# Narrow attention's Newton steps and step orders: drains replaced by a chained semaphore, new orders on every engine

## The chip, the cores and the metric

One core of one Trainium2 chip. The metric is device time of one execution in microseconds (us), lower is better. The kernel before took 7786.44 us, the median of 3 runs (7783.06 to 7791.43).

## The reference, cut to what matters

The whole kernel is a stack of four mixer and feed blocks over 8 sequences of 512 tokens with 128 channels, float32. The change touches one of them, the feed of block 0 (names that begin with L0f in the profile): a local attention net of depth 6 with 16 heads of 64 channels and windows of 32 tokens. Cut down:

```python
def attn_layer(x, Wqkv, qs, ksc, Wo):
    q, k, v = split(x @ Wqkv)                 # 16 heads x 64 each
    q = q / max(norm(q), 1e-12) * qs          # also k
    q = q * cos * scale + rotate_half(q) * sin * scale
    k = k * cos / scale + rotate_half(k) * sin / scale
    out = local_attention(q, k, v)            # own and previous 32 tokens, softmax
    return out @ Wo

def ffn_layer(x, g, bln, W1, b1, W2, b2):
    xn = layernorm(x) * g + bln
    a, gate = split(xn @ W1 + b1)
    return a * gelu(gate) @ W2 + b2
```

Each layer's two halves are preceded by a shift of half the channels by one token, and each adds to x. The change touches how 1 / norm is reached (three Newton steps on an integer guess) and in which order everything is issued, not what is computed.

## The kernel before, in words

`narrow_attention_net` (L354) cuts a sequence into four tiles (tt = 0 to 3) of 128 tokens. One pass of the main stage handles one sequence of one layer: 6 layers by 8 sequences, 48 passes, written out without loops. Two short stages of the same code stand around it, one that fills the pipeline and one that empties it.

Every engine has an order of its own. TensorE's is written by hand: `ORDER` (L381) lists one tile's steps, `SIDE` (L385) puts the ten steps of the feed half and of the next sequence's input at one of three places, (tile, place), `tile_steps` expands both. A step of TensorE for tile tt works on different tiles of the data:

- `q`, `k` (i = 0 or 1): projection of 8 heads for tile tt + 2, L1110, two recorded matmuls. `v`: the same for tile tt + 1.
- `tq`, `tk`: four transposes (L1116) of the rotated and scaled q or k of tile tt + 1.
- `score` u: a mask matmul (L1129) and 64 small recorded matmuls (L1135). `flip` u: four transposes of the probabilities (L1143). `value` u: 64 small recorded matmuls (L1165). `oturn` u: four transposes of the result (L1171). `out`: 16 recorded matmuls with Wo (L1182). `value 1`, `oturn 1` and `out` are one tile behind.
- sides: `shift` (L1099) and `fshift` (L1191 to L1193), the shifted inputs of the two halves; `fturn` (L1198); `gate` and `up` 0 to 2 (L1205); `down` (L1211).

Steps of the kinds in `RING` write one of four PSUM banks in turn: a step's bank is that of the ring step four before it, and it waits until that one has been read out.

The other engines' orders are computed. `in_order` (L461) walks over TensorE's steps and adds up `TOOK`; each step calls for events on the other engines (`act_events`, `dve_events`, `pool_events`), and each event is due at its step's end plus a delay from `LATER` (main stage) or `PLAIN` (the other two). An engine's order is that of the due times, and within it each engine runs strictly in order.

What a q or k projection calls for: ScalarE copies it (L890) and squares it (L895); VectorE multiplies the swapped halves by sine, which also empties the PSUM bank (`rot`, L993), and sums the squares per head (`ssq`, L1001); GpSimd multiplies by cosine (`cos`, L849) and adds (`add`, L856). The buffers for the sine product and the squares are two deep. After a tile's last q or k comes `newton` (L1002 to L1017) on VectorE: eleven operations on 128 x 32 elements, each a true dependency of the one before it, with `e.drain()` ahead of each, and a count of the semaphore `normed` at the end. GpSimd then multiplies q and k by the result (`scale` 0 and 1, L862), for which the turns one tile later wait.

What a score calls for: `max` (L1022) and `sub` (L1027) on VectorE, the exponential on ScalarE (L918), `total` (L1033) with a reciprocal (L1036) on VectorE. `sub` waits for the count of `max`. What a value calls for: `onorm` (L1043) on VectorE, for which `oturn` waits. `fshift` calls for a copy and the statistics on VectorE (L1056 to L1062), `rstd` on GpSimd (L866 to L872) and `xn` on ScalarE (L936).

Of the kernel before, what the change touches and what calls it, by code (L numbers as in the profile page):

```python
# [9 lines left out]
I32 = mybir.dt.int32  # L10
# [343 lines left out]
def narrow_attention_net(nc, g, name, heads, depth, w):  # L354
# [19 lines left out]
    def turn(tt, what, c):  # L374
# [6 lines left out]
    ORDER = [("side", 0), ("value", 1), ("score", 0), ("q", 0), ("k", 1), ("oturn", 1), ("score", 1), ("q", 1), ("flip",  # L381
             0), ("out", 0), ("v", 1), ("k", 0), ("side", 1), ("value", 0), ("v", 0), ("tq", 0), ("side", 2), ("tk", 1),
             ("tq", 1), ("flip", 1), ("oturn", 0), ("tk", 0)]
    BEHIND = {("value", 0): 0, ("value", 1): 1, ("oturn", 0): 0, ("oturn", 1): 1, ("out", 0): 1}
    SIDE = [(("fshift",), (0, 1)), (("fturn",), (1, 1)), (("gate", 0), (1, 2)), (("gate", 1), (1, 2)), (("gate", 2), (2,  # L385
            0)), (("up", 0), (2, 2)), (("shift",), (0, 2)), (("up", 1), (2, 0)), (("up", 2), (2, 1)),
            (("down",), (3, 0))]
# [90 lines left out]
    def dve_events(step, D):  # L478
        kind = step[0]
        if kind == "proj" and step[2] != "v":  # L480
            found = [(D["rot"], ("rot",) + step[1:]), (D["ssq"], ("ssq",) + step[1:])]
            if step[2:] == QK_ORDER[-1]:
                found.append((D["newton"], ("newton", step[1])))
            return found
# [10 lines left out]
    def pool_events(step, D):  # L495
# [10 lines left out]
        if kind == "fshift":  # L506
# [3 lines left out]
    PLAIN = {"exp": 1.5, "unflip": 0.3, "ocopy": 0.3, "xn": 2.0, "act_ring": 0.2, "copy": 0.2, "square": 1.0, "ssq": 2.0, "rot": 1.2, "newton":  # L510
             3.0, "max": 0.2, "sub": 0.2 + 0.6, "total": 5.0, "onorm": 0.5, "norm_gap": 2.0, "unflip_dve": 0.5, "dve_ring": 0.3, "cos": 1.0, "add": 2.5,
             "scale": 6.0, "scale_gap": 2.0, "rstd": 2.0}
    LATER = {"exp": 4.11, "unflip": 1.88, "ocopy": 1.76, "xn": 9.48, "act_ring": 1.83, "copy": 2.05, "square": 2.48,
             "ssq": 3.92, "rot": 3.52, "newton": 9.41, "max": 1.06, "sub": 3.3, "total": 5.73, "onorm": 4.32, "norm_gap":
             14.0, "unflip_dve": 6.64, "dve_ring": 1.85, "cos": 3.51, "add": 4.27, "scale": 11.99, "scale_gap": 0.54,
             "rstd": 4.39}
# [3 lines left out]
    with ExitStack() as ctx:  # L520
# [58 lines left out]
        def programs(r, STEPS):  # L579
# [7 lines left out]
            for _, tt, what, c in QK:  # L587
                assert place["ssq", tt, what, c] < place["newton", tt]
# [17 lines left out]
            made_by = lambda steps, kind: [s[1:] for s in steps if s[0] == kind]  # L606
            until_layer = lambda steps: steps[:steps.index(("layer",))] if ("layer",) in steps else []
# [3552 lines left out]
```

## Time and profile before

| what | value |
|---|---|
| median of 3 runs | 7786.44 us |
| profiled execution | 7796.52 us |
| its span | 7794.6 us |
| main stage of the narrow attention | from about 668 us to 4240 us |
| TensorE busy, whole span | 82% |
| VectorE, ScalarE, GpSimd busy | 73%, 55%, 60% |

The profile is one execution, seen instruction by instruction. PE is TensorE (PEld its weight loads), DVE VectorE, ACT ScalarE, POOL GpSimd, SP the engine that issues the DMAs. Each engine executes in its order, so the time between two starts on an engine is the price of the first with all its waits; a matmul's recorded end is modelled, and matmuls overlap, so starts are the surer reading. L numbers are lines of the kernel before.

### The profile page before, as it was taken

How to read it: one execution, taken by the hardware profiler on the slowest of the kernel's cores; microseconds unless marked ns; L12 is line 12 of the kernel's file. 1: busy time of each engine (PE TensorE's matmuls, PEld its weight loads, DVE VectorE, ACT ScalarE, POOL GpSimd, SP SyncE). 2: the span in 40 equal slices, each digit the busy share in tenths (PEclk: the TensorE clock that was granted, in tenths of full speed). 3: DMA queues.
4: the chain of work that ended last, by engine and by line, in shares of the span. 5: the costliest groups of instructions: out<-in, count | busy, mean ns of one | idle time of the engine just before them, and what ended most of it. 6: DMA issues, size and time to landing. Idle time of an engine off the chain costs nothing. (4 is left out here: it accounts for less than half of the span.)

```text
span 7794.6 us, 241834 instructions
## 1 busy us (share of the span) xinstructions
PE 6366.5 (82%) x93078; PEld 4343.4 (56%) x93078; DVE 5662.3 (73%) x11712; ACT 4278.5 (55%) x7973; POOL 4672.3 (60%) x3762
## 2 busy tenths in 40 slices
PE   5776999999999999999998599977888757734268
PEld 2333666666666666666665588874555423322256
DVE  6885888888887888888886477766777668853533
ACT  5553666666666666666665344436777655512012
POOL 5776777777777777777776254544444357723000
PEclk8888999999999999999999799999999978867579
DMA  3332112112112112112111200001110033333001
GB/s 116 123 135 57 50 47 66 47 51 64 48 51 60 51 47 63 50 50 61 50 51 39 70 6 6 6 20 27 23 31 23 17 134 126 132 121 87 10 14 33
DMA packets 344463, 440.90 MB, mean 57 GB/s; under 512 B 151976, under 2 KB 235648, under 8 KB 324416
## 3 DMA queue, kind: packets, MB, share of 16 engines
q1 hardware_dynamic: 335632, 405.19, 17.0%
q8 instruction: 759, 12.44, 0.7%
q10 hardware_dynamic: 1584, 15.21, 0.5%
q0 software_dynamic: 6144, 5.25, 0.4%
q14 instruction: 344, 2.82, 0.1%
HBM read 217.42 MB, written 42.14 MB: 33 GB/s over the span
## 5 line engine op out<-in xcount | busy, mean ns | idle before, releaser
L1110 PE MATMUL L0f_ring<-L0f_wqkv,L0f_hT 128*128 128x512 f32 x2324 | 1196.5, 624 | 20.5 <-issue 18.0
L849 POOL TENSOR_TENSOR L0f_qr<-L0f_qs,L0f_table 128x512 f32<-128x512 f32 x776 | 990.8, 1277 | 216.7 <-issue 115.1
L856 POOL TENSOR_TENSOR L0f_qr<-L0f_qr,L0f_m 128x512 f32<-128x512 f32 x776 | 989.3, 1275 | 138.0 <-issue 119.6
L862 POOL TENSOR_TENSOR L0f_qr<-L0f_qr,L0f_rn 128x1024 f32<-128x1024 f32 x388 | 752.0, 1959 | 422.3 <-DVE L0f_rn L1016 400.3
L890 ACT ACTIVATE L0f_qs<-L0f_ring 128x512 f32<-128x512 f32 x776 | 460.1, 593 | 625.0 <-PE L0f_ring L1110 618.1
L993 DVE TENSOR_TENSOR L0f_m<-L0f_ring,L0f_table 128x512 f32<-128x512 f32 x776 | 531.4, 685 | 46.2 <-ACT L0f_qs L890 14.5
L1001 DVE TENSOR_REDUCE L0f_ssq<-L0f_sq 128x8 f32<-128x512 f32 x776 | 528.1, 681 | 29.6 <-ACT L0f_sq L895 13.7
L1110 PEld LDWEIGHTS L0f_ring<-L0f_wqkv,L0f_hT 128*128 128x128 f32 x2324 | 382.1, 190 | 266.9 <-issue 210.5
L895 ACT ACTIVATE L0f_sq<-L0f_qs 128x512 f32<-128x512 f32 x776 | 492.0, 634 | 36.0 <-DVE L0f_ssq L1001 4.2
L1116 PEld LDWEIGHTS L0f_ring<-const_ident,L0f_qr 128*128 128x128 f32 x3088 | 361.8, 141 | 178.2 <-issue 170.5
L1116 PE MATMUL L0f_ring<-const_ident,L0f_qr 128*128 128x128 f32 x3088 | 428.2, 274 | 16.6 <-POOL L0f_qr L862 16.6
L1022 DVE TENSOR_REDUCE L0f_mx<-L0f_scores 128x8 f32<-128x512 f32 x384 | 265.6, 692 | 165.5 <-PE L0f_scores L1135 160.5
L1182 PE MATMUL L0f_ring<-L0f_wo,L0f_oT 128*128 128x128 f32 x3088 | 382.5, 277 | 2.9 <-issue 2.1
L2475 PE MATMUL L0a_y<-L0a_hc,const_ident 128*128 128x512 f32 x512 | 288.6, 698 | 108.3 <-DVE L0a_hc L2396 86.7
L1165 PEld LDWEIGHTS L0f_scores<-L0f_vmix,L0f_pT 64*32 64x32 f32 x18480 | 264.7, 105 | 190.8 <-issue 185.0
L1182 PEld LDWEIGHTS L0f_ring<-L0f_wo,L0f_oT 128*128 128x128 f32 x3088 | 362.2, 193 | 10.0 <-issue 3.6
L1135 PE MATMUL L0f_scores<-L0f_kT,L0f_qT 64*32 64x64 f32 x24576 | 337.3, 224 | 36.9 <-issue 36.9
L2475 PE MATMUL L2a_y<-L2a_hc,const_ident 128*128 128x512 f32 x512 | 283.5, 687 | 101.3 <-DVE L2a_hc L2396 85.1
L904 ACT ACTIVATE L0f_vb<-L0f_ring 128x512 f32<-128x512 f32 x386 | 230.5, 597 | 246.7 <-PE L0f_ring L1110 246.4
L2255 POOL TENSOR_TENSOR L0a_dbu<-L0a_du,L0a_bc_all 128x512 f32<-128x512 f32 x256 | 325.3, 1304 | 57.1 <-DVE L0a_du L2375 50.2
L2255 POOL TENSOR_TENSOR L2a_dbu<-L2a_du,L2a_bc_all 128x512 f32<-128x512 f32 x256 | 325.3, 1304 | 54.6 <-DVE L2a_du L2375 50.7
L1165 PE MATMUL L0f_scores<-L0f_vmix,L0f_pT 64*32 64x64 f32 x18480 | 324.2, 224 | 34.4 <-SPq L155 10.3
(533 smaller groups left out, 17157.9 us busy)
## 6 DMA issues: line engine op xcount, KB each, us to landing
L0f_vmix<-L0f_vb SPq DMA_DIRECT2D x768, 128.0 KB
L0a_bc_all<-L0a_bc_rows SPq DMA_DIRECT2D x32, 2048.0 KB, 11.2
L2a_bc_all<-L2a_bc_rows SPq DMA_DIRECT2D x32, 2048.0 KB, 11.0
L0f_vmix<-L0f_vb SPq DMA_DIRECT2D x672, 64.0 KB
L1f_vmix<-L1f_vb SPq DMA_DIRECT2D x96, 128.0 KB, 2.3
L0f_wqkv<-L_ffn_wqkv_dram SPq DMA_DIRECT2D x7, 1536.0 KB, 6.0
L2f_parts<-L2f_zero ACTq DMA_DIRECT2D x8, 1088.0 KB, 12.7
n_s<-mixer_out SPq DMA_DIRECT2D x32, 256.0 KB, 4.9
```

The lines of the kernel that those rows point to most:

```text
L849: e.tensor_tensor(rotated, qs[:, q % QN], spread(cos, 1, 8), ALU.mult).then_inc(cosed.sem, 1)
L856: e.tensor_tensor(rotated, rotated, m2[:, q % SN], ALU.add).then_inc(added.sem, 1)
L862: e.tensor_tensor(rotated, rotated, spread(rn[:, tt, 2 * c:2 * c + 2], 3, DH), ALU.mult).then_inc(scaled.sem, 1)
L895: e.activation(sq[:, q % SN], qs[:, q % QN], ACT.Square).then_inc(squared.sem, 1)
L993: e.tensor_tensor(m2[:, q % SN].rearrange("p h (a d) -> p h a d", a=2), swapped, spread(sin, 1, 8).rearrange("p h (a d) -> p h a d", a=2), ...
L1001: e.tensor_reduce(ssq[:, tt % 2, slot(step)], sq[:, q % SN], AX.X, ALU.add).then_inc(summed.sem, 1)
L1110: e.matmul(bank[:], hT[:, buffer_of(it, step), tt * P:tt * P + P], wqkv[:, layer % 2, col:col + 512], start=True, stop=True).then_inc(full, 1)
L1116: a = e.transpose(bank[:, j * P:j * P + P], qr[:, tt % 2, 2 * c + "qk".index(what), 2 * j:2 * j + 2, :], g.ident[:])
L1165: a = e.matmul(o_ps[cols, s, h, j], pT[half, s, j, cols], values, start=True, stop=True)
L1182: a = e.matmul(bank[:, 0:C], oT[:, tt % 2, j, :], wo[:, j, :], start=j == 0, stop=j == pairs - 1)
L2255: e.tensor_tensor(dbu[:, s], du[:, par, d], bc_all[:, n // QN, 0, n % QN], ALU.mult).then_inc(dbu_ready.sem, 1)
L2475: e.matmul(y_ps[:, d], g.ident[:], hc[:, (2 * n + d) % 4], start=n == 0, stop=n == states - 1).then_inc(added.sem, 1)
```

## The change

The eleven operations of `newton` become eleven steps, each with a due time of its own (`newton` plus i times `newton_gap`), so that other steps of VectorE can fall between them. The drains go: step i waits for the count that step i - 1 leaves in the new semaphore `stepped`, step 0 for the tile's last `ssq`; step 10 counts `normed`. `ORDER`, `SIDE` and the delays `LATER` are replaced.

```diff
-    ORDER = [("side", 0), ("value", 1), ("score", 0), ("q", 0), ("k", 1), ("oturn", 1), ("score", 1), ("q", 1), ("flip",
-             0), ("out", 0), ("v", 1), ("k", 0), ("side", 1), ("value", 0), ("v", 0), ("tq", 0), ("side", 2), ("tk", 1),
-             ("tq", 1), ("flip", 1), ("oturn", 0), ("tk", 0)]
+    ORDER = [("value", 1), ("side", 0), ("k", 1), ("score", 0), ("q", 0), ("oturn", 1), ("score", 1), ("v", 1), ("q", 1),
+             ("flip", 0), ("out", 0), ("k", 0), ("side", 1), ("value", 0), ("v", 0), ("flip", 1), ("tq", 0), ("tk", 0),
+             ("side", 2), ("oturn", 0), ("tq", 1), ("tk", 1)]
-    SIDE = [(("fshift",), (0, 1)), (("fturn",), (1, 1)), (("gate", 0), (1, 2)), (("gate", 1), (1, 2)), (("gate", 2), (2,
-            0)), (("up", 0), (2, 2)), (("shift",), (0, 2)), (("up", 1), (2, 0)), (("up", 2), (2, 1)),
-            (("down",), (3, 0))]
+    SIDE = [(("fshift",), (0, 2)), (("fturn",), (1, 1)), (("gate", 0), (2, 0)), (("gate", 1), (2, 0)), (("gate", 2), (2,
+            0)), (("up", 0), (2, 1)), (("shift",), (0, 1)), (("up", 1), (2, 1)), (("up", 2), (2, 1)), (("down",), (2, 2))]
...
-                found.append((D["newton"], ("newton", step[1])))
+                found += [(D["newton"] + D["newton_gap"] * i, ("newton", step[1], i)) for i in range(11)]
...
-    LATER = {"exp": 4.11, "unflip": 1.88, "ocopy": 1.76, "xn": 9.48, "act_ring": 1.83, "copy": 2.05, "square": 2.48,
-             "ssq": 3.92, "rot": 3.52, "newton": 9.41, "max": 1.06, "sub": 3.3, "total": 5.73, "onorm": 4.32, "norm_gap":
-             14.0, "unflip_dve": 6.64, "dve_ring": 1.85, "cos": 3.51, "add": 4.27, "scale": 11.99, "scale_gap": 0.54,
-             "rstd": 4.39}
+    LATER = {"exp": 3.43, "unflip": 2.66, "ocopy": 2.24, "xn": 8.29, "act_ring": 2.88, "copy": 0.93, "square": 2.98,
+             "ssq": 4.36, "rot": 2.48, "newton": 5.91, "newton_gap": 0.22, "max": 1.12, "sub": 1.55, "total": 4.54,
+             "onorm": 2.65, "norm_gap": 14.0, "unflip_dve": 6.33, "dve_ring": 1.0, "cos": 5.86, "add": 5.9, "scale": 13.61,
+             "scale_gap": 4.95, "rstd": 1.96}
...
-            normed = r.count("normed", made_by(DVE_STEPS, "newton"))
+            stepped = r.count("stepped", [s for s in made_by(DVE_STEPS, "newton") if s[1] < 10])
+            normed = r.count("normed", [s[:1] for s in made_by(DVE_STEPS, "newton") if s[1] == 10])
...
-                            tt = step[1]
+                            tt, i = step[1:]
                             flat = lambda t: t.rearrange("p c h -> p (c h)")
                             z, t, out = flat(ssq[:, tt % 2]), flat(est[:]), flat(rn[:, tt])
-                            e.drain()
-                            e.tensor_scalar(z, z, 1e-24, None, ALU.max)
-                            e.drain()
-                            e.tensor_scalar(out.bitcast(I32), z.bitcast(I32), -0.5, float(0x5F3759DF), ALU.mult, ALU.add)
-                            for i in range(3):
-                                e.drain()
-                                e.scalar_tensor_tensor(t, out, -0.5, out, ALU.mult, ALU.mult)
-                                e.drain()
-                                e.tensor_tensor(t, t, z, ALU.mult)
-                                e.drain()
+                            if i:
+                                e.wait_ge(*stepped(it, (tt, i - 1)))
+                            else:
+                                e.wait_ge(*summed(it, LAST_SSQ[tt]))
+                            if i == 0:
+                                a = e.tensor_scalar(z, z, 1e-24, None, ALU.max)
+                            elif i == 1:
+                                a = e.tensor_scalar(out.bitcast(I32), z.bitcast(I32), -0.5, float(0x5F3759DF), ALU.mult, ALU.add)
+                            elif i % 3 == 2:
+                                a = e.scalar_tensor_tensor(t, out, -0.5, out, ALU.mult, ALU.mult)
+                            elif i % 3 == 0:
+                                a = e.tensor_tensor(t, t, z, ALU.mult)
+                            else:
                                 a = e.scalar_tensor_tensor(out, t, 1.5, out, ALU.add, ALU.mult)
-                            a.then_inc(normed.sem, 1)
+                            a.then_inc(normed.sem if i == 10 else stepped.sem, 1)
```

## Rows read from the trace of the kernel before

**Rows 1.** Busy by window: start:end, length, PE, PEld, DVE, ACT, POOL, PE clock, DMA
```profile
2000.00:3000.00 1000.00, 955.39 (x17970) 657.60 (x17969) 818.24 (x1819) 674.29 (x1226) 781.47 (x592) 1.00 0.19 52
```

**Rows 2.** Instructions on tile hT: ns min/median/max, first to last start
```profile
L885 ACT ACTIVATE L0f_hT<-L0f_ring x49: 598/599/601, 634.5 to 4178.3; 128x512 f32<-128x512 f32 x49
```

**Rows 3.** Waits of PE, 760 to 4170 us: total us, times, longest us
```profile
PE L0f_ring L1099 <- DVE L0f_m L993: 40.9, 46, 1.2
PE L0f_scores L1135 <- issue: 34.6, 27, 2.2
PE L0f_scores L1143 <- ACT L0f_prob L918: 22.6, 44, 0.8
```

**Rows 4.** Timeline of PE in one pass: start, us, instruction [idle before]
```profile
853.05 1.13 PE L1110 MATMUL L0f_ring<-L0f_wqkv,L0f_hT 128*128 128x512 f32 x2
854.01 0.60 PE L1116 MATMUL L0f_ring<-const_ident,L0f_qr 128*128 128x128 f32 x4
855.48 0.66 PE L1099 MATMUL L0f_ring<-const_ident,L0f_xs 128*128 128x128 f32 x4 [0.87 <-DVE L0f_m L993]
...
857.28 0.60 PE L1171 MATMUL L0f_ring<-const_ident,L0f_os 128*128 128x128 f32 x4
857.72 0.60 PE L1116 MATMUL L0f_ring<-const_ident,L0f_qr 128*128 128x128 f32 x4
859.40 0.38 PE L1129 MATMUL L0f_scores<-L0f_mask,ident_bf 128*128 128x256 bf16 x2
859.71 0.86 PE L1135 MATMUL L0f_scores<-L0f_kT,L0f_qT 64*32 64x64 f32 x64
860.50 1.98 PE L1110 MATMUL L0f_ring<-L0f_wqkv,L0f_hT 128*128 128x512 f32 x4
862.32 0.60 PE L1171 MATMUL L0f_ring<-const_ident,L0f_os 128*128 128x128 f32 x4
```

**Rows 5.** Timeline of PE later in the same pass, to the next pass's fshift
```profile
882.82 1.12 PE L1110 MATMUL L0f_ring<-L0f_wqkv,L0f_hT 128*128 128x512 f32 x2
884.46 0.66 PE L1143 MATMUL L0f_scores<-const_ident,L0f_prob 128*128 128x128 f32 x4 [0.51 <-ACT L0f_prob L918]
...
916.52 0.63 PE L1171 MATMUL L0f_ring<-const_ident,L0f_os 128*128 128x128 f32 x4
...
921.27 1.88 PE L1110 MATMUL L0f_ring<-L0f_wqkv,L0f_hT 128*128 128x512 f32 x4
923.31 0.67 PE L1191 MATMUL L0f_ring<-f,const_ident 128*128 128x256 f32 x2 [0.15 <-DVE f L1051]
```

**Rows 6.** Timeline of DVE, the last Newton operation of a tile and what follows
```profile
914.94 0.19 DVE L1016 SCALAR_TENSOR_TENSOR L0f_rn<-L0f_est,L0f_rn 128x32 f32<-128x32 f32 x1
915.09 0.69 DVE L1022 TENSOR_REDUCE L0f_mx<-L0f_scores 128x8 f32<-128x512 f32 x1
915.69 0.68 DVE L1043 TENSOR_TENSOR L0f_os<-L0f_scores,L0f_sums 128x512 f32<-128x512 f32 x1
```

**Rows 7.** Groups of DVE, 760 to 4170 us: count, busy us, mean ns, idle before
```profile
L1012 DVE SCALAR_TENSOR_TENSOR L0f_est<-L0f_rn 128x32 f32<-128x32 f32 x555 | 188.3, 339 | 44.5 <-issue 3.6
L1036 DVE RECIPROCAL L0f_sums<-L0f_sums 128x8 f32<-128x8 f32 x370 | 75.2, 203 | 34.4 <-issue 0.9
```

**Rows 8.** Timeline of ACT, a copy and the square that waits for it
```profile
923.25 0.60 ACT L890 ACTIVATE L0f_qs<-L0f_ring 128x512 f32<-128x512 f32 x1 [0.26 <-PE L0f_ring L1110]
923.94 0.63 ACT L895 ACTIVATE L0f_sq<-L0f_qs 128x512 f32<-128x512 f32 x1
```

**Rows 9.** Timelines of DVE and ACT: fshift's copy, the next rot, and xn
```profile
924.84 0.69 DVE L1056 COPY L0f_xn<-L0f_ring 128x512 f32<-128x512 f32 x1 [0.79 <-PE L0f_ring L1193]
...
927.14 0.69 DVE L993 TENSOR_TENSOR L0f_m<-L0f_ring,L0f_table 128x512 f32<-128x512 f32 x1 [0.19 <-issue]
...
932.76 1.65 ACT L936 ACTIVATE L0f_xn<-L0f_xn,L0f_shifted,L0f_rstd 128x128 f32<-128x128 f32 x4 [1.06 <-POOL L0f_shifted L872]
```

**Rows 10.** Waits of POOL, 760 to 4170 us: total us, times, longest us
```profile
POOL L0f_qr L862 <- DVE L0f_rn L1016: 384.5, 176, 4.3
```

More of the change, by code:

```diff
@@ L508, in pool_events @@
         return []
-    PLAIN = {"exp": 1.5, "unflip": 0.3, "ocopy": 0.3, "xn": 2.0, "act_ring": 0.2, "copy": 0.2, "square": 1.0, "ssq": 2.0, "rot": 1.2, "newton":
-             3.0, "max": 0.2, "sub": 0.2 + 0.6, "total": 5.0, "onorm": 0.5, "norm_gap": 2.0, "unflip_dve": 0.5, "dve_ring": 0.3, "cos": 1.0, "add": 2.5,
+    PLAIN = {"exp": 1.5, "unflip": 0.3, "ocopy": 0.3, "xn": 2.0, "act_ring": 0.2, "copy": 0.2, "square": 1.0, "ssq": 2.0, "rot": 1.2, "newton": 3.0, "newton_gap": 0.01, "max": 0.2, "sub": 0.2 + 0.6, "total": 5.0, "onorm": 0.5, "norm_gap": 2.0, "unflip_dve": 0.5, "dve_ring": 0.3, "cos": 1.0, "add": 2.5,
              "scale": 6.0, "scale_gap": 2.0, "rstd": 2.0}
-    LATER = {"exp": 4.11, "unflip": 1.88, "ocopy": 1.76, "xn": 9.48, "act_ring": 1.83, "copy": 2.05, "square": 2.48,
-             "ssq": 3.92, "rot": 3.52, "newton": 9.41, "max": 1.06, "sub": 3.3, "total": 5.73, "onorm": 4.32, "norm_gap":
-             14.0, "unflip_dve": 6.64, "dve_ring": 1.85, "cos": 3.51, "add": 4.27, "scale": 11.99, "scale_gap": 0.54,
-             "rstd": 4.39}
+    LATER = {"exp": 3.43, "unflip": 2.66, "ocopy": 2.24, "xn": 8.29, "act_ring": 2.88, "copy": 0.93, "square": 2.98,
+             "ssq": 4.36, "rot": 2.48, "newton": 5.91, "newton_gap": 0.22, "max": 1.12, "sub": 1.55, "total": 4.54,
+             "onorm": 2.65, "norm_gap": 14.0, "unflip_dve": 6.33, "dve_ring": 1.0, "cos": 5.86, "add": 5.9, "scale": 13.61,
+             "scale_gap": 4.95, "rstd": 1.96}
     RING = ("shift", "proj", "turn", "oturn", "out", "fshift", "fturn", "gate", "up", "down")
@@ L587, in programs @@
             for _, tt, what, c in QK:
-                assert place["ssq", tt, what, c] < place["newton", tt]
+                assert place["ssq", tt, what, c] < place["newton", tt, 0]
                 assert place["cos", tt, what, c] < place["add", tt, what, c]
@@ L606, in programs @@
             made_by = lambda steps, kind: [s[1:] for s in steps if s[0] == kind]
+            LAST_SSQ = {s[0]: s for s in made_by(DVE_STEPS, "ssq")}
             until_layer = lambda steps: steps[:steps.index(("layer",))] if ("layer",) in steps else []
```

## The prediction

> **What bounds the kernel now.** TensorE is busy 82% of the span, but that is a mean over stages. I read first the window in the middle of the stage that the change touches: TensorE 95.5% busy, VectorE 82%, GpSimd 78%, ScalarE 67%, with TensorE's clock fully granted, its upper level of 2.4 GHz [rows 1]. The stage is 48 passes; between the first and the last copy of hT lie 48 of them and 3543.8 us, so 73.83 us a pass [rows 2], and a microsecond in the pass is 48 in the kernel. Then the waits of TensorE over 46 passes [rows 3], and the timeline of one pass for what they really cost, from start to start [rows 4, 5].
>
> What the reader is to see in the starts. After four transposes the next step starts 0.44 us later (857.28 to 857.72). The shift starts 1.47 after such a group (854.01 to 855.48), so it lost 1.03 [rows 4]; 46 waits, one a pass [rows 3]. Its bank is that of projection k0, which VectorE empties only behind fshift's copy and statistics (924.84 to 927.14, one pass on) [rows 9]. Value 1 stands directly behind turn k0 and too soon behind flip 1, and score 0 waits for turn k0's copy: 857.72 + 0.44 + 0.79 (64 small matmuls, 859.71 to 860.50) is 858.95, yet the mask matmul starts at 859.40, 0.45 lost [rows 4]. Tile 0 begins in the same way, so I count 0.8 a pass. A single projection ahead of transposes takes 0.96 (853.05 to 854.01), a double one 1.82 (860.50 to 862.32) [rows 4]. So flip 0 of tile 2, at 884.46 instead of 882.82 + 0.96, lost 0.68, waiting for an exponential [rows 5]; 44 waits say once a pass [rows 3]. fshift starts 2.04 after a double projection (921.27 to 923.31) instead of 1.82, behind the output's addition: 0.22 lost [rows 5]. And inside the small matmuls of score stand 27 holes without a releaser, 34.6 us in 46 passes, 0.75 a pass, up to 2.2 us each [rows 3]. Together 3.5 of 73.83.
>
> The holes stand only in score, the densest part of TensorE's program. The Trainium skill, Runtime: NRT & Kernel Launch, section Instruction fetch mechanics, says that fetching is hidden because instructions are dispatched more slowly than they are refilled. By that density is not their cause and they would all stay, which is one end of my term below; no row here names their cause.
>
> **The drains.** A small operation of the chain takes 0.19 us [rows 6] and has 0.08 idle ahead of it (44.5 us over 555) [rows 7]: 0.27 apart. In the new chain each waits for a count of the same engine instead; the trace does not show that for these operations. Lower end: independent long operations start 0.60 apart at 0.69 long (915.09 to 915.69), an overlap of 0.09 [rows 6], which a dependency should exclude. Nearest row: ScalarE's square, which waits for its copy by a count and starts 0.09 after it ends (923.25 + 0.60 to 923.94) [rows 8]. I take 0.09 against 0.08: 44 operations a pass, 0.4 us more of VectorE; the lower end would be 44 times 0.17, 7.5 less. So the drains' removal gains nothing. The Trainium skill, VectorE: DVE Perf Modes, section Rules for kernel authors, advises saving operations and not semaphores in a chain, since the flush comes anyway; by that rule too this part is worth 0.
>
> **The spreading.** I worked out VectorE's new order from ORDER, TOOK and LATER. Eleven due times 0.22 apart are 2.2 wide and meet hardly anything: in tile 0 fshift falls between the second and third step, in tile 2 onorm 0 between the fourth and fifth, in tiles 1 and 3 all eleven stand together. So the spreading is there in name only. It would not be on TensorE's path either: the chain ends before GpSimd's scale, which waited 384.5 us for it [rows 10], and the turns use scale's result most of a tile later. What it costs: max and sub now stand together with a wait between, where onorm or rot lay between them: 8 pairs a pass at 0.09 + 0.09, 1.4 us more of VectorE.
>
> **TensorE's order, taken away.** Shift comes right after k0; its bank is v1's, which ScalarE empties early: 1.03 gone. Five steps now part flip 1 from value 1, and score 0 has a projection ahead: 0.8 gone. fshift is far behind the output's addition: 0.22 gone. For flip 0 of tile 2, k1 and v1 now lie between the gates and it, but all three gates come at once on ScalarE: half of 0.68, 0.34. Value 1 and score 0, 260 small instructions in a row, are parted by k1: of the holes' 0.75 between nothing and all goes, I take half, 0.38. Together 2.8.
>
> **Added.** By 0.96 and 1.82 a second projection in a row costs 0.86, so each change from projection to transposes is 0.10 [rows 4]. Pairs q0 k1 and v1 k0 are split and v1 q1 is joined: one change more a tile, 0.4 a pass. A projection ahead of the mask matmul is in no row; 0 and 0.15 are its ends, 0.10 the nearest. Net 2.4.
>
> **VectorE's lateness.** A tile of TensorE without sides is some 14.7 us (11 to 12 in projections, transposes and scores as above, and two values and the output). VectorE's tile: 16 long operations at 0.60 [rows 6], 9.6; two reciprocals at 0.20 with a gap of 0.09 on either side [rows 7], 0.9 with what they keep from overlapping; the output's addition, 0.2; Newton, 11 times 0.27 and what slow ones add (L1012 alone 0.15 in the mean, three times a tile [rows 7]), about 4; two subs, 0.3: 15.0. The sides now pile up in tile 2 (gates, ups, down: some 8 us of TensorE for 4 of VectorE), and tiles 3, 0 and 1 run bare: TensorE 44.1 + 2.3 = 46.4, VectorE 45.0 + 2.3 for fshift [rows 9] = 47.3. Before, down and two gates lay in tiles 3 and 1. To that comes ScalarE: xn takes 1.65 and waited 1.06 for GpSimd [rows 9]; fshift moves 3.5 us later on TensorE, and behind ssq and two Newton steps on VectorE, xn only behind one copy more. Copies and squares queue behind that wait, rot and ssq behind them: 0.5 to 1. So VectorE falls 1.4 to 1.9 behind by tile 1. Its slack: today oturn 1 starts at 916.52, as soon as onorm 1 is done at 916.37 [rows 5, 6]; in the new order onorm comes ahead of max, which gives back 0.6. I charge 1.0 of new wait on oturn 1, between 0 and 2.
>
> GpSimd stays covered: busy 58 of 73.8 us a pass [rows 1], with 8 of waiting for Newton to give up [rows 10].
>
> **Sum.** 2.4 - 1.0 = 1.4 a pass, times 48: 67 us. The profiled execution took 7796.52, so 7729; the median stood 10 below it, so 7719.
>
> **Rivals.**
> 1. All goes well: no new wait, all of 0.68 and of the holes gone: 1.03 + 0.8 + 0.22 + 0.68 + 0.75 - 0.4 = 3.1, times 48 = 148: 7638. For it: TensorE hangs on VectorE by few links. Against: three bare tiles. Chance 0.13.
> 2. The orders only move the waits: 2.4 a pass of new ones, 7786. The drains alone would give this too, 0.4 us of VectorE being nothing. Chance 0.13.
> 3. Slower, by VectorE at the step from tile 0 to 1. fshift stands inside the Newton chain; if it is late the chain waits, onorm 1 and rot k1 come after it, and oturn 1 stops TensorE. It decides from 2.4 us of new wait. Small operations are sometimes slow; the mean of L1012 is 0.15 above 0.19 [rows 6, 7], which one in six at 1.1 would make (an estimate). Two such in tiles 0 and 1 each make 3.6, less 1.1 that the slack of tile 2 and the holes take back, plus my 1.0: 3.5, so 1.1 times 48 = 53: 7839. For it: GpSimd lags more when scale 1 is put between later steps. Against: tile 2 lets VectorE recover 3 us. Chance 0.24.
>
> The forecast has 0.50.
>
> **How the numbers follow.** A measurement of this kernel can tell 0.2% (16 us) from no change. Forecast and rival 1 are faster: 0.63; rival 2 is within: 0.13; rival 3 slower: 0.24. The forecast's own range is 7680 (new wait 0.2) to 7770. For 8 in 10 it reaches from 7650, near rival 1, to 7830, most of rival 3.
>
> **What would show it.** Right: the wait of L1099 on L993 gone, those of L1143 and L1165 smaller, new waits of L1171 on L1043, a pass of 72.4 us, Newton operations still 0.27 apart. Wrong: Newton chains cut by long operations or under 2.8 us; as many holes in L1135 as before; L1143 waiting over 1 us in tile 1; a pass over 74 us. If TensorE's waits vanish and the pass stays, my prices from start to start are wrong.

## The result, and the profile after

The kernel after takes 7588.7 us, the median of 4 runs (7580.1 to 7590.9), against 7788.9 us beside it on the same chip: ratio 0.974, 95% interval 0.9723 to 0.9757. The forecast was 7719 with a range of 7650 to 7830, so the time lies below the range, and below the best rival (7638).

The profiled execution took 7590.9 us with a span of 7588.9. The lines are those of before, with numbers three higher: L1113 is the projection, L1119 the turns, L1138 score, L1146 flip, L1168 value, L1174 oturn, L1194 to L1196 fshift; on VectorE L1011 to L1019 are Newton, L1025 max, L1030 sub, L1046 onorm, L1054 the output's addition, L1059 fshift's copy, L1077 and L1081 the feed's last two additions.

The instructions on tile hT, as in [rows 2] (min/median/max ns, first to last start):

```profile
L885 ACT ACTIVATE L0f_hT<-L0f_ring x49: 577/579/597, 634.2 to 3983.3; 128x512 f32<-128x512 f32 x49
```

The difference of the two starts is 3349.1 us over 48 passes, 69.77 us a pass where it was 73.83. That is 4.06 less, and 48 times this is 195 of the 200 us. So nearly all of it comes from the one stage. The window of [rows 1] (columns: length, PE, PEld, DVE, ACT, POOL, granted clock, DMA share, GB/s):

```profile
2000.00:3000.00 1000.00, 996.60 (x19160) 699.43 (x19159) 912.60 (x1929) 715.96 (x1302) 827.12 (x629) 1.00 0.21 58
```

TensorE is busy 99.7% of it (95.5% before) and VectorE 91% (82%): more passes lie in the window, and more of VectorE's small operations are slow (below). All waits of TensorE from 760 to 3960 us, the view of [rows 3] (total us, times, longest us):

```profile
PE L0f_scores L1138 <- issue: 3.0, 9, 0.5
PE L0f_ring L1174 <- DVE L0f_os L1046: 2.1, 7, 0.6
PE L0f_scores L1146 <- ACT L0f_prob L918: 1.4, 5, 0.3
PE L0f_ring L1113 <- ACT L0f_qT L911: 0.3, 1, 0.3
```

Together 7 us, where the whole list of before, of which [rows 3] show three, sums to 125: the shift's wait (40.9), the flips' (22.6) and the holes (34.6) of [rows 3] are gone but for 4.4 us, and the wait of oturn on onorm that I charged at 1.0 us a pass is 2.1 us in all. TensorE's timeline in a pass (start, us) shows the one cost that was added:

```profile
2002.31 1.13 PE L1113 MATMUL L0f_ring<-L0f_wqkv,L0f_hT 128*128 128x512 f32 x2
2003.28 0.38 PE L1132 MATMUL L0f_scores<-L0f_mask,ident_bf 128*128 128x256 bf16 x2
```

Here a projection ahead of the mask matmul takes 0.97 from start to start, 0.11 more than the 0.86 of a projection ahead of another; over all 184 of the stretch the mean is 0.94, 0.08 more. The forecast had 0.10. VectorE's timeline, with one line of GpSimd's, shows what the chained semaphore does:

```profile
2004.85 0.68 DVE L1025 TENSOR_REDUCE L0f_mx<-L0f_scores 128x8 f32<-128x512 f32 x1
2005.56 0.70 DVE L1030 TENSOR_TENSOR L0f_scores<-L0f_scores,L0f_mx 128x512 f32<-128x512 f32 x1
...
2014.98 1.27 POOL L856 TENSOR_TENSOR L0f_qr<-L0f_qr,L0f_m 128x512 f32<-128x512 f32 x1 [0.16 <-issue]
2015.11 1.20 DVE L1015 SCALAR_TENSOR_TENSOR L0f_est<-L0f_rn 128x32 f32<-128x32 f32 x1
2016.34 0.19 DVE L1017 TENSOR_TENSOR L0f_est<-L0f_est,L0f_ssq 128x32 f32<-128x32 f32 x1
2016.56 0.19 DVE L1019 SCALAR_TENSOR_TENSOR L0f_rn<-L0f_est,L0f_rn 128x32 f32<-128x32 f32 x1
2016.79 0.19 DVE L1015 SCALAR_TENSOR_TENSOR L0f_est<-L0f_rn 128x32 f32<-128x32 f32 x1
...
2030.54 0.18 DVE L1013 TENSOR_SCALAR L0f_rn<-L0f_ssq 128x32 int32<-128x32 int32 x1
2032.06 0.69 DVE L1059 COPY L0f_xn<-L0f_ring 128x512 f32<-128x512 f32 x1 [1.34 <-PE L0f_ring L1196]
2032.84 0.87 DVE L1062 BATCH_NORM_STATS2 L0f_stats<-L0f_xn 128x6 f32<-128x128 f32 x4
...
2034.28 0.23 DVE L1015 SCALAR_TENSOR_TENSOR L0f_est<-L0f_rn 128x32 f32<-128x32 f32 x1
```

Small Newton operations start 0.22 to 0.23 apart, not 0.27: each starts 0.03 us after the one it waits for ends. The same 0.03 stands between max and the sub that waits for its count. fshift's copy and statistics stand inside the chain, behind its second step. What my expectations below call fshift's addition is this group.

The first Newton operation shown takes 1.20 us, not 0.19. It begins while GpSimd's addition (L856) runs and ends some 0.05 after it (2015.11 + 1.20 = 2016.31, against 2014.98 + 1.27 = 2016.25). That is the rule in the whole trace: of the 2134 Newton operations of after, 336 take over 0.5 us, every one of them began while a multiplication by cosine (L849) or that addition (L856) of GpSimd was running, and each ended 0.035 to 0.054 us after it. None of the 1022 that overlap nothing of GpSimd's is slow. In before it is 246 of 2134, with 0.034 to 0.056. So the slow form reads as a wait for GpSimd's instruction to end, and it counts as busy: the 91% hold this waiting.

### The profile page after: what moved, and what is told of

It is laid out like the page before. It is cut to its first block and busy times, and to the rows that moved or that the text cites. A ratio compares the mean times of both kernels' runs of the same rounds, so it can differ in the third digit from the quotient of the medians.

```text
span 7588.9 us, 239593 instructions
## 1 busy us (share of the span) xinstructions
PE 6306.7 (83%) x93014; PEld 4349.8 (57%) x93078; DVE 5801.0 (76%) x11712; ACT 4272.6 (56%) x7973; POOL 4662.0 (61%) x3762
## 5 line engine op out<-in xcount | busy, mean ns | idle before, releaser
L1113 PE MATMUL L0f_ring<-L0f_wqkv,L0f_hT 128*128 128x512 f32 x2324 | 1236.0, 628 | 15.9 <-issue 10.8
L849 POOL TENSOR_TENSOR L0f_qr<-L0f_qs,L0f_table 128x512 f32<-128x512 f32 x776 | 988.2, 1273 | 141.1 <-issue 89.6
L856 POOL TENSOR_TENSOR L0f_qr<-L0f_qr,L0f_m 128x512 f32<-128x512 f32 x776 | 988.7, 1274 | 125.8 <-issue 123.2
L1113 PEld LDWEIGHTS L0f_ring<-L0f_wqkv,L0f_hT 128*128 128x128 f32 x2324 | 369.1, 190 | 208.4 <-issue 132.8
L1119 PE MATMUL L0f_ring<-const_ident,L0f_qr 128*128 128x128 f32 x3088 | 402.1, 273 | 16.7 <-POOL L0f_qr L862 16.7
L1119 PEld LDWEIGHTS L0f_ring<-const_ident,L0f_qr 128*128 128x128 f32 x3088 | 350.4, 141 | 18.4 <-issue 18.4
L1168 PEld LDWEIGHTS L0f_scores<-L0f_vmix,L0f_pT 64*32 64x32 f32 x18480 | 267.9, 106 | 140.8 <-issue 140.4
L1168 PE MATMUL L0f_scores<-L0f_vmix,L0f_pT 64*32 64x64 f32 x18480 | 330.7, 224 | 16.5 <-SPq L155 9.8
L1138 PE MATMUL L0f_scores<-L0f_kT,L0f_qT 64*32 64x64 f32 x24576 | 333.5, 224 | 3.3 <-issue 3.0
L1168 PE MATMUL L0f_scores<-L0f_vb,L0f_pT 64*32 64x64 f32 x6160 | 333.6, 225 | 0.0
```

The costliest lines, as they stand in the source:

```text
L849: e.tensor_tensor(rotated, qs[:, q % QN], spread(cos, 1, 8), ALU.mult).then_inc(cosed.sem, 1)
L856: e.tensor_tensor(rotated, rotated, m2[:, q % SN], ALU.add).then_inc(added.sem, 1)
L1113: e.matmul(bank[:], hT[:, buffer_of(it, step), tt * P:tt * P + P], wqkv[:, layer % 2, col:col + 512], start=True, stop=True).then_inc(full, 1)
L1119: a = e.transpose(bank[:, j * P:j * P + P], qr[:, tt % 2, 2 * c + "qk".index(what), 2 * j:2 * j + 2, :], g.ident[:])
L1168: a = e.matmul(o_ps[cols, s, h, j], pT[half, s, j, cols], values, start=True, stop=True)
```

## The experiments

Each ratio is to the kernel before on the same chip, with its 95% interval; "pass" is from the instructions on hT as above. A waits view of an experiment covers 760 to 3960 us, some 43 to 46 passes. ORDER and SIDE also set the due times, so an edit of either reorders the other engines too; the first two edits below, of drains and chain alone, leave every engine's order as it was. Line numbers differ by up to five between kernels; the tile names tell which line is meant.

| kernel | median us | ratio | pass us |
|---|---|---|---|
| after | 7588.7 | 0.9740 (0.9723 to 0.9757) | 69.77 |
| after, with drains | 7669.4 | 0.9841 (0.9823 to 0.9859) | 71.22 |
| before, with the chain | 7815.6 | 1.0028 (1.0018 to 1.0037) | 74.35 |
| the same, last addition from PSUM | 7788.0 | 0.9983 (0.9974 to 0.9993) | 73.60 |
| after, with the old delays | 7755.3 | 0.9952 (0.9934 to 0.9970) | 73.18 |
| before, with chain and new delays | 7816.7 | 1.0023 (1.0012 to 1.0033) | 74.21 |
| before, shift and fshift moved | 7769.2 | 0.9962 (0.9949 to 0.9974) | 73.12 |
| before, k 1 between value 1 and score 0 | 7893.2 | 1.0125 (1.0108 to 1.0142) | 75.89 |
| after, with the old sides | 7733.4 | 0.9918 (0.9899 to 0.9938) | 72.61 |
| after, score 0 ahead of k 1 | 7700.3 | 0.9866 (0.9850 to 0.9881) | 72.00 |
| after, reciprocals chained too | 7589.8 | 0.9727 (0.9714 to 0.9741) | 69.74 |
| after, gap 0 | 7764.0 | 0.9957 (0.9941 to 0.9974) | 73.29 |
| after, gap 0.8 | 7764.4 | 0.9958 (0.9942 to 0.9975) | 73.19 |
| after, gap 0, fshift ahead of the chain | 7658.0 | 0.9817 (0.9797 to 0.9838) | 71.06 |
| after, gap 0, fshift and onorm 20 ahead | 7618.1 | 0.9763 (0.9742 to 0.9784) | 70.23 |

**The drains put back.** Orders, sides and delays of after; only the chain's waits are replaced:

```diff
-                            if i:
-                                e.wait_ge(*stepped(it, (tt, i - 1)))
-                            else:
-                                e.wait_ge(*summed(it, LAST_SSQ[tt]))
+                            e.drain()
```

> The changed kernel with a drain ahead of each of the eleven Newton steps in place of the semaphore chain; all orders stay. In the profile after, a chained step starts 0.03 us after the one before it ends, a drained one before started 0.08 after: 44 steps a pass, 2 us of VectorE. Theory A (TensorE's new path made the gain, VectorE still idles 2.6 us a pass): 7589 to 7625 us. Theory B (VectorE is so full that the cheaper chain carries the gain): the 2 us come back on TensorE's path, 48 times, 7670 to 7690.

7669, at the lower edge of theory B's range. The waits of TensorE, first row, and below it the group of the Newton operation that [rows 7] show:

```profile
PE L0f_ring L1171 <- DVE L0f_os L1043: 47.5, 60, 1.5
```

```profile
L1012 DVE SCALAR_TENSOR_TENSOR L0f_est<-L0f_rn 128x32 f32<-128x32 f32 x540 | 229.9, 426 | 56.3 <-issue 11.1
```

The same group in the kernel after:

```profile
L1015 DVE SCALAR_TENSOR_TENSOR L0f_est<-L0f_rn 128x32 f32<-128x32 f32 x552 | 236.3, 428 | 22.9 <-issue 0.2
```

Idle ahead of each is 0.10 us with drains (56.3 over 540) and 0.04 with the chain (22.9 over 552), at an equal mean of 0.43 us busy. With drains oturn 1 waits 47.5 us for onorm, 1.06 a pass over the 45 in this stretch, in the place and of the size that the forecast charged. From start to start it costs a little more: the four projections of a pass that stand ahead of oturn 1 take 5.28 us with drains and 3.95 with the chain, and these 1.33 are most of the 1.45 between the two passes (71.22 and 69.77). So the chain is worth 80 us (7669.4 - 7588.7) on these orders, and nine tenths of it are this one wait.

**The chain alone.** Orders and old delays of before, the chain with gap 0.

```diff
-                            e.drain()
+                            e.wait_ge(*stepped(it, (tt, i - 1)))
```

> The semaphore chain alone: TensorE's order, the sides and the delays are those of before, with the eleven steps due at one time. Theory A: TensorE's waits of before (shift, value, score, flip) don't hang on the Newton chain, so 7770 to 7789 us. Theory B: 2 us of VectorE a pass are worth up to 96 us, 7690 to 7720.

It is 0.28% slower, which neither theory had. Lines of its timeline:

```profile
890.16 3.76 POOL L863 TENSOR_TENSOR L0f_qr<-L0f_qr,L0f_rn 128x1024 f32<-128x1024 f32 x2 [3.18 <-DVE L0f_rn L1020]
891.75 0.69 DVE L1078 TENSOR_TENSOR L0f_y<-L0f_ring,L0f_b 128x512 f32<-128x512 f32 x1 [1.67 <-PE L0f_ring L1215]
892.53 1.93 DVE L1082 TENSOR_TENSOR f<-L0f_y,f 128x512 f32<-128x512 f32 x1
895.16 0.68 DVE L1047 TENSOR_TENSOR L0f_os<-L0f_scores,L0f_sums 128x512 f32<-128x512 f32 x1
895.99 0.63 PE L1175 MATMUL L0f_ring<-const_ident,L0f_os 128*128 128x128 f32 x4 [0.46 <-DVE L0f_os L1047]
```

Newton ends sooner, GpSimd's scale starts sooner, and one of its two multiplications now runs when the feed's last addition begins. This adds two tiles in SBUF and takes 1.93 us instead of 0.69. onorm and oturn behind it are late: oturn waits 20.2 us in all, 0.47 a pass. The instructions on tile f, min/median/max ns, of the kernel before and of this one:

```profile
L1078 DVE TENSOR_TENSOR f<-L0f_y,f x49: 691/694/1834, 750.8 to 4276.3; 128x512 f32<-128x512 f32 x49
```

```profile
L1082 DVE TENSOR_TENSOR f<-L0f_y,f x49: 691/1928/1935, 746.6 to 4300.3; 128x512 f32<-128x512 f32 x49
```

**The same with one operand in PSUM.** This kernel leaves out the bias b2: its last addition reads the bank in PSUM instead of the tile y in SBUF. The addition into y still runs, and the bank is given free one addition later (the lines shown leave this out).

```diff
-                            e.tensor_tensor(x2, y[:], x2, ALU.add).then_inc(x2_ready.sem, 1)
+                            e.tensor_tensor(x2, ring.at(step).rearrange("p (t c) -> p t c", t=TT), x2,
+                                            ALU.add).then_inc(x2_ready.sem, 1)
```

> The chain alone on the orders of before, but the feed half's last addition reads its sum from PSUM and not from a second tile in SBUF (it leaves out the bias b2). With the chain alone that addition took 1.93 us instead of 0.69, since Newton ended sooner and the addition then met GpSimd's second scale, and oturn 1 of tile 3 waited 0.6 us longer. Theory D (two SBUF operands beside GpSimd make it slow): the addition takes 0.7 us, the wait of oturn (L1175) on onorm falls from 20 us to under 5, and the kernel is back at 7770 to 7795 us. Rival E (any operation beside scale is slow, or the wait has another cause): 1.9 us again and 7805 to 7825.

The last addition's instructions on tile f:

```profile
L1082 DVE TENSOR_TENSOR f<-L0f_ring,f x49: 690/692/692, 744.5 to 4263.6; 128x512 f32<-128x512 f32 x49
```

No instance is slow any more though GpSimd's multiplication runs beside 48 of the 49, no wait of oturn on onorm is left, and 0.45% comes back: theory D. The Trainium skill, GPSIMD Engine Reference, section Specifications, says that GpSimd's path to SBUF is shared with VectorE and contended by instructions with two SBUF inputs; this pair agrees, 1.93 us against 0.69. The traces also show the size. The 48 slow additions of the kernel with the chain alone, the 14 of before and 48 of the 49 in after end 0.544 to 0.549 us after the multiplication of GpSimd that ran when they began; the 34 quick ones of before began with only 0.13 or 0.14 of it left. So the price is the rest of GpSimd's instruction, and a different start makes it anything from nothing to 1.2 us. In after it is paid in full, where it holds up nothing:

```profile
L1081 DVE TENSOR_TENSOR f<-L0f_y,f x49: 693/1836/1840, 744.9 to 4081.7; 128x512 f32<-128x512 f32 x49
```

**The order alone.** ORDER and SIDE of after with the chain, but the LATER of before, a gap of 0 among them.

```diff
-             "ssq": 4.36, "rot": 2.48, "newton": 5.91, "newton_gap": 0.22, "max": 1.12, "sub": 1.55, "total": 4.54,
...
+             "ssq": 3.92, "rot": 3.52, "newton": 9.41, "newton_gap": 0.0, "max": 1.06, "sub": 3.3, "total": 5.73, "onorm": 4.32, "norm_gap":
...
```

> TensorE's new order and sides with the old delays, so that VectorE, ScalarE and GpSimd are ordered by the delays of before. Theory A in its strong form (TensorE's order alone): 7589 to 7620 us. Rival C (the delays matter, since fshift's statistics and max stand ahead of what TensorE waits for): half of the gain is lost, 7660 to 7740, with new waits of oturn (L1174) on onorm.

All of its waits of TensorE:

```profile
PE L0f_ring L1174 <- DVE L0f_os L1046: 86.1, 175, 1.3
PE L0f_scores L1146 <- ACT L0f_prob L918: 14.2, 44, 0.8
PE L0f_scores L1168 <- ACT L0f_pT L923: 13.3, 43, 0.7
PE L0f_scores L1138 <- issue: 1.6, 6, 0.3
```

Shift, fshift and the holes are mended, and four oturns a pass wait for onorm instead: 86 us. It went theory C's way, and further than its 7740.

**The delays alone.** Chain and new LATER on the old ORDER and SIDE.

> TensorE's old order and sides with the new delays and the chain. Theory A: the wait of shift, those of value and score behind turn k0 and the holes in score all belong to TensorE's order and stay: 7750 to 7800 us. Rival C: a good part of the gain comes with the delays alone, below 7740.

7817, above the 7800 of theory A: no gain, and 0.23% slower than before. Shift still waits 37.9 us, the holes are 30.4, and oturn's wait on onorm is 26.8 us where before has 3.3.

**Shift and fshift moved in before.**

```diff
-    SIDE = [(("fshift",), (0, 1)), (("fturn",), (1, 1)), (("gate", 0), (1, 2)), (("gate", 1), (1, 2)), (("gate", 2), (2,
-            0)), (("up", 0), (2, 2)), (("shift",), (0, 2)), (("up", 1), (2, 0)), (("up", 2), (2, 1)),
+    SIDE = [(("fshift",), (0, 2)), (("fturn",), (1, 1)), (("gate", 0), (1, 2)), (("gate", 1), (1, 2)), (("gate", 2), (2,
+            0)), (("up", 0), (2, 2)), (("shift",), (0, 1)), (("up", 1), (2, 0)), (("up", 2), (2, 1)),
```

> The kernel before, drains and delays too, with shift and fshift changed over as in the new sides: shift right after k0, fshift where shift was. Theory A (shift waited for rot of k0 behind fshift's statistics): the wait of L1099 on L993 is gone, 1.0 us a pass, 7735 to 7755. Rival F (VectorE is so full that it waits elsewhere: fshift's statistics now stand between onorm 0 and Newton and xn comes later): 7775 to 7800, with more wait of oturn or flip in tile 1.

The first of its waits of TensorE:

```profile
PE L0f_ring L1171 <- DVE L0f_os L1043: 38.8, 45, 1.6
PE L0f_scores L1135 <- issue: 36.2, 26, 2.1
```

The shift's 40.9 us (0.89 a pass) are gone and oturn takes 38.8 (0.88): as the second rival had it for the whole change, a wait moved. The net is 0.71 us a pass, between the two theories; the forecast's prices for these two steps alone were 1.03 and 0.22.

**One step moved, and the holes.** In before, k 1 between value 1 and score 0; and in after, the reverse.

```diff
-    ORDER = [("side", 0), ("value", 1), ("score", 0), ("q", 0), ("k", 1), ("oturn", 1), ("score", 1), ("q", 1), ("flip",
+    ORDER = [("side", 0), ("value", 1), ("k", 1), ("score", 0), ("q", 0), ("oturn", 1), ("score", 1), ("q", 1), ("flip",
```

> The kernel before with one step moved: k 1 stands between value 1 and score 0, so that the two groups of 64 small matmuls are parted, and all else is as before (drains too). Theory H (the holes in score come from the two groups in a row): issue idle in score falls from 34.6 us to under 10. With nothing given back the time is 7750 to 7765; with VectorE giving it back, 7765 to 7800. Theory I (the holes are not a matter of what stands next to score): 25 to 40 us of holes remain, and the time is 7780 to 7830.

The first of its waits of TensorE:

```profile
PE L0f_ring L1171 <- DVE L0f_os L1043: 72.2, 169, 0.7
PE L0f_scores L1143 <- ACT L0f_prob L918: 47.3, 42, 1.4
PE L0f_ring L1099 <- DVE L0f_m L993: 37.3, 42, 1.2
PE L0f_scores L1135 <- issue: 21.5, 23, 1.4
```

```diff
-    ORDER = [("value", 1), ("side", 0), ("k", 1), ("score", 0), ("q", 0), ("oturn", 1), ("score", 1), ("v", 1), ("q", 1),
+    ORDER = [("value", 1), ("side", 0), ("score", 0), ("k", 1), ("q", 0), ("oturn", 1), ("score", 1), ("v", 1), ("q", 1),
```

> The changed kernel with k1 behind score 0, so that value 1 and score 0 stand next to each other again, as before. Theory G (260 small matmuls in a row make the holes): 30 us or so of L1138 waiting for nothing in 43 passes come back (after: 3 us), and the time goes up by 20 to 60 us. Rival H (the holes had to do with waits ahead of value and score, or with DMA traffic): the holes stay at 3 us; what the time does then is VectorE's new order, max ahead of onorm, as in the run with the old delays.

The same view of this one:

```profile
PE L0f_ring L1174 <- DVE L0f_os L1046: 21.1, 37, 0.9
PE L0f_scores L1168 <- ACT L0f_pT L923: 21.0, 42, 0.6
PE L0f_scores L1168 <- DVE f L1054: 19.0, 48, 0.7
PE L0f_scores L1138 <- issue: 13.6, 16, 1.7
```

Parted in before, the holes fall from 0.75 us a pass to 0.51 (21.5 over 42 passes); put together in after, they rise from 0.07 to 0.31 (13.6 over 44). Kernels that share TensorE's order differ too: those with the ORDER of before have 0.70 to 0.88 a pass, those with that of after 0.02 to 0.18. So the neighbour matters, but it explains about a third either way, and all four theories missed.

The place of a hole shows more than its neighbours do. Count the records on TensorE from the start of the trace, matmuls, weight loads and those of its sequencer together. Of the 34 stretches of idle time without a releaser in before, in score and elsewhere (760 to 4170 us), 33 begin at the 26th to 28th record of a block of 256; in after it is 9 of 9, in the parted kernel 25 of 25, in the dense one 19 of 19. So the holes stand at one fixed place in the blocks. Of these places, 184 of before lie in score and 27 have a hole; 189 of after do and 9 have one; of the 185 of before in value none has. An edit of the order changes which matmuls lie at these places and how fast TensorE comes to them. That a block of instructions came late is the plain reading, but no run here moved the places alone, so it is not shown, nor what makes one place in seven a hole.

Both kernels mostly show something else: one step of TensorE moved by a microsecond, with the due times that follow from it, costs 1.25% and 1.3% in new waits for VectorE and ScalarE.

**The old sides in after.** Only SIDE is put back.

> The kernel after with only SIDE put back: shift and fshift change places, two gates move from tile 2 to tile 1 and down from tile 2 to tile 3. Theory P (my forecast's: the sides piled in tile 2 leave three bare tiles and cost VectorE lateness, so balance helps or is free): 7560 to 7600. Theory T (the sides stand where they do because their results are then ready, and the freed ring banks fit: back in the old places shift waits for its bank again): 7640 to 7740, with a wait on shift of 0.5 to 1 us a pass or new waits on the gates' first matmul.

The first of its waits of TensorE:

```profile
PE L0f_ring L1195 <- DVE f L1055: 43.9, 43, 1.4
PE L0f_ring L1120 <- DVE L0f_m L994: 19.7, 44, 0.8
PE L0f_ring L1120 <- ACT L0f_gate L950: 16.9, 44, 0.4
```

7733, in theory T's range, though by other waits than it named: fshift now stands one place nearer to the output whose addition it needs (1.0 us a pass), and turns wait for banks. The sides piled in tile 2 had left no wait in after that a balance could give back; what the balance alone costs was not tried, as shift and fshift moved with it.

**VectorE made faster still.** In after, the two drains around each reciprocal become counted waits.

```diff
-                            e.drain()
-                            e.reciprocal(total, total)
-                            e.drain()
+                            e.wait_ge(*totaled(it, key))
+                            e.reciprocal(total, total).then_inc(inverted.sem, 1)
```

> The changed kernel with the two drains around each reciprocal replaced too: the reciprocal waits for the count of its sum, and onorm for the count of its reciprocal. By the gaps of the profile after (drains 0.09 and 0.08, a counted wait 0.03) it takes about 0.2 us off each of 8 a pass, 1.7 us of VectorE. Theory A (TensorE's own path is left, some 0.5 us of waits a pass): 7570 to 7589 us. Theory B (VectorE still holds TensorE up): 7510 to 7560.

7589.8, the same as after (7588.7; the ratios' intervals overlap), pass 69.74 against 69.77. Busy by window, columns as above:

```profile
2000.00:3000.00 1000.00, 996.86 (x19101) 698.97 (x19095) 903.20 (x1930) 717.19 (x1305) 827.38 (x630) 1.00 0.21 57
```

VectorE is busy 9 us less in the window and TensorE's 99.7% stays. In after TensorE's own path is the bound, so the same kind of edit that was worth 80 us is now worth nothing that can be measured.

**The spreading.** The forecast said that it is there in name only. The kernel after with other gaps:

```diff
-             "newton_gap": 0.22,
+             "newton_gap": 0.0,
```

> The kernel after with newton_gap 0 in place of 0.22: all eleven steps of a chain are due at once, so fshift's addition (tile 0) and onorm 0 (tile 2) come behind the whole chain instead of inside it. Theory A (spreading is nothing; TensorE's own path is the bound): within 0.2% of the kernel after, 7575 to 7605, pass 69.7 to 70.0 us. Theory S (the few long operations inside the chain are what the spreading is for: without them fshift's transposes or oturn 0 wait): 7620 to 7680, with a new wait of 0.6 to 2 us a pass on fshift's matmuls or on oturn.

> The kernel after with newton_gap 0.8: the chain's steps are now really spread, with max, sub, onorm and rot of neighbouring steps between them. Theory A (VectorE has slack, so its order within a few us is free): 7575 to 7610. Theory L (each step that falls next to a long operation hides its own start, but the chain ends some 5 us later and GpSimd's scale and the copies behind it follow late): 7620 to 7800, with a larger wait of GpSimd's scale on Newton's last operation (251 us in the kernel after) and new waits of TensorE's q and k turns.

Both lost 175 us, seven eighths of what the change had brought. TensorE's first two waits with gap 0:

```profile
PE L0f_ring L1113 <- DVE L0f_xn L1059: 64.5, 44, 2.1
PE L0f_ring L1174 <- DVE L0f_os L1046: 37.5, 48, 1.2
```

And with gap 0.8:

```profile
PE L0f_ring L1119 <- DVE L0f_m L993: 41.2, 44, 1.2
PE L0f_ring L1113 <- DVE L0f_m L993: 27.2, 77, 0.7
```

And two of the waits of VectorE and GpSimd with gap 0.8:

```profile
DVE L0f_m L993 <- POOL L0f_qr L856: 130.8, 170, 1.5
POOL L0f_qr L862 <- DVE L0f_rn L1019: 451.3, 175, 5.1
```

With gap 0 the copy that empties fshift's bank stands behind all eleven steps. That bank is the one of k 1 in tile 1, four ring steps on (oturn 0, tq 1, tk 1, k 1), and the projection waits for it. With 0.8 it is theory L: the chain ends later, so GpSimd's scale waits 451 us for it (251 in after), GpSimd's additions behind it are late, and rot, which needs the sine buffer that they free, waits 131 us for them (1.0 in after) and then empties TensorE's banks late. Is it the division, then, or only the place of the two groups that lie in a chain, fshift's in tile 0 and onorm 0 in tile 2 ("onorm 20")? Two kernels keep every chain whole and delay it:

```diff
-             "ssq": 4.36, "rot": 2.48, "newton": 5.91, "newton_gap": 0.22, "max": 1.12, "sub": 1.55, "total": 4.54,
+             "ssq": 4.36, "rot": 2.48, "newton": 6.40, "newton_gap": 0.0, "max": 1.12, "sub": 1.55, "total": 4.54,
```

> The kernel after with newton_gap 0 and the delay newton 6.40 in place of 5.91: every chain is undivided; fshift's addition stands ahead of the whole chain of tile 2's q and k instead of behind its second step, onorm 20 behind the whole chain of tile 0's instead of behind its fourth step; all else on VectorE, ScalarE and GpSimd is in the same order. Theory N (the spreading itself is nothing, what counts is that fshift's addition does not stand behind the chain): 7580 to 7630, the wait of the projection L1113 on fshift's copy L1059 (64.5 us with gap 0) gone. Theory S (the division is what counts): 7680 to 7780.

> As e13_fshift_ahead, with the delay newton 6.80, so that onorm 20 also stands ahead of its undivided chain. Theory N: 7575 to 7605, within 0.2% of the kernel after, with no wait of TensorE over 5 us. Theory S: 7680 to 7780. If the two kernels differ by over 30 us, onorm 20 behind the chain (0.46 us a pass on oturn with gap 0) is a term of its own.

TensorE's largest wait with fshift alone ahead:

```profile
PE L0f_ring L1174 <- DVE L0f_os L1046: 42.4, 92, 1.2
```

And with both ahead:

```profile
PE L0f_ring L1174 <- DVE L0f_os L1046: 15.2, 48, 0.7
```

The times lie between the two theories, 7658 and 7618. fshift ahead brings 106 of the 175 us back, onorm 20 ahead another 40. 18 us (by the ratios) to 29 (by the medians) are left to the kernel after; the intervals overlap, so by the times alone this last part is not shown. VectorE's waits show where it may come from. The first row with both ahead:

```profile
DVE L0f_xn L1059 <- PE L0f_ring L1196: 98.7, 46, 2.2
```

And the first two of the kernel after:

```profile
DVE L0f_m L993 <- ACT L0f_qs L890: 52.2, 119, 1.0
DVE L0f_xn L1059 <- PE L0f_ring L1196: 48.9, 46, 1.6
```

VectorE waits 2.15 us a pass for fshift's matmuls when its copy comes first, and 1.06 when two Newton steps are done in that time. So the place is most of it, and the division saves VectorE 1.1 us of waiting a pass. The traced passes differ by 0.46 (70.23 against 69.77), which would be the part that reached TensorE; this last link is argued.

## Why the prediction was wrong

The forecast took 1.4 us a pass off, and it was 4.06. By its own steps:

- **"So the drains' removal gains nothing."** This step failed, and with it the sum. It priced a counted wait on VectorE by ScalarE's row, 0.09 [rows 8], against the drain's 0.08 [rows 7]. Measured on VectorE it is 0.03. Eleven steps a tile make 44 times 0.045, 2.0 us less of VectorE a pass, where I had 0.4 more. Max and sub side by side cost 0.03 and the lost overlap, some 0.9 for eight pairs and not 1.4. With the drains left in, the kernel takes 7669, inside the range; the chain's 1.45 us a pass is the larger part of the 2.66 that the forecast missed, and the other 1.21 are TensorE's: its terms below were some 1.6 too small, and the wait on oturn with drains, 1.4 from start to start, took 0.4 more than was charged.
- **"I charge 1.0 of new wait on oturn 1."** With drains the view gives 1.06 a pass, where it was put. But this wait was made of VectorE's lateness, and the two microseconds above take it away: 0.05 is left. The two steps are one error: a price off by 0.05 us decided whether the second engine was behind the first. The forecast held the two terms apart, and the range did not take in the lower end that the text itself gave for the drains ("7.5 less"). The rule of the Trainium skill that the forecast took to make this part worth 0 (VectorE: DVE Perf Modes, Rules for kernel authors) speaks of a pipeline flush behind every operation and of semaphores, not of drain instructions that the kernel issues itself; stretched to these, it is not borne out: the operations are the same, and semaphores in place of drains are worth 80 us.
- **The holes, 0.38 of 0.75.** 0.07 are left, so 0.68 went. The Trainium skill, Runtime: NRT & Kernel Launch, section Instruction fetch mechanics, has blocks of 256 instructions, and says that crossing from one to the next is mostly hidden; the blocks agree with the places of the holes, and "mostly hidden" with most of these places and not with the 0.75 us a pass of before. The forecast took from it that all holes would stay, as one end of its term; nearly all went. What makes a single hole stays open.
- **Flip 0 of tile 2, 0.34 of 0.68.** All went: 22.6 us became 1.4.
- **The rest.** TensorE shed 4.46 us of stalls a pass (4.06, and 0.4 that the switches were to add). The stalls that the forecast had found make 3.4 of it; about 1.0 it had not. Holes in a projection (L1110, 6.5 us in the list of waits of before, 0.14 a pass) were left out. By the starts of all passes the double projections ahead of oturn 1 took, in two of the four tiles, 0.11 and 0.16 longer in the mean than the 1.82 I had from one pass (holes not counted): one timeline was too few. The remaining 0.6 was not traced.
- **Right:** the waits of L1099, of value and score behind flip 1, and of fshift are gone, and a switch costs about the 0.10 that was put.
- **Spreading "in name only":** the description holds (chains whole but for two places), the valuation does not. I asked whether the chain was on TensorE's path, and it was not; what stands behind the chain on VectorE was. Of the 175 us lost with gap 0, 146 hang on whether fshift's group and onorm 20 stand ahead of the chain or behind it.
- **Rival 2** (waits only move) is close to what each part does alone: order -0.5% (with the chain), delays with chain +0.2%, chain +0.3%. **Rival 3** (fshift in the chain stops oturn) has it backwards: with fshift in the chain oturn waits 2.1 us in all, and fshift behind the chain is what stops TensorE. Rival 3's slow small operations are real, more of them than before (336 against 246), and cost TensorE nothing. Rival 1 was nearest, and missed the gain of the chain.

Of the forecast's own signs, the pass of 72.4, the new waits on onorm and "Newton operations still 0.27 apart" all came out otherwise; the last is the one that names the cause.

## What to carry to other kernels

When a second engine is close behind the first (here 2 us of VectorE a pass decided), terms for it are not additive: first work out which of the two is late in each case, then take the larger. Replace explicit drains in a chain of small dependent operations by a count where that engine is near the bound, and do not expect it to help where it is not. A chain of small operations that is off the critical path still has to be placed by what is queued behind it: ahead of work that releases a buffer it cost TensorE 1.5 us a pass here (64.5 us over 44), and two steps done inside a wait took no time of VectorE's. Orders, delays and waits of such a kernel have to be changed together: here order, delays or chain alone gave 0.5% or less, orders with delays and the old drains 1.6%, all together 2.6%. Before two operations of VectorE and GpSimd are ordered next to each other, look at what the one reads while the other runs.

## What the runs showed of the hardware

- A counted wait on the engine's own last instruction costs VectorE 0.03 us, a drain 0.08, ScalarE's copy and square 0.09.
- An addition of two SBUF tiles (128x512, float32) takes 0.69 us alone. Begun while GpSimd multiplies, it ends 0.55 us after that multiplication: up to 1.93 us in all. With one operand in PSUM it stays at 0.69.
- A Newton operation on 128x32 elements that begins under GpSimd's multiplication by cosine or its addition ends 0.03 to 0.06 us after it: 0.19 becomes up to 1.3. None begun and ended beside an idle GpSimd is slow.
- Finishing sooner made the kernel slower by that collision (before, with the chain).
- Idle time of TensorE without a releaser begins at the same record of a block of 256, in 33 of 34 cases before and 9 of 9 after. Its sum inside score is 34.6, 21.5, 13.6 and 3.0 us in four orders, and 1.0 to 8.0 in kernels that share the order of after.
